# Softmax rows of two of four heads turned on VectorE in 32x32 blocks and put together by DMAs inside SBUF, instead of on TensorE

## What is computed

```python
# _L3_xattn_ref; _L2_xattn_ref has its own layernorm, a bias and a gate besides
q = (query @ w_q).reshape(B, Q, HEADS, HEAD_DIM).transpose(0, 2, 1, 3)
k = (key @ w_k).reshape(B, Kl, HEADS, HEAD_DIM).transpose(0, 2, 1, 3)
v = (value @ w_v).reshape(B, Kl, HEADS, HEAD_DIM).transpose(0, 2, 1, 3)
scores = jnp.einsum('bhqd,bhkd->bhqk', q, k) * scale
attn = jax.nn.softmax(scores, axis=-1)
out = jnp.einsum('bhqk,bhkd->bhqd', attn, v)
out = out.transpose(0, 2, 1, 3).reshape(B, Q, HEADS * HEAD_DIM)
return out @ w_o
```

## Time and profile before

| | |
|---|---|
| runs | 1220.64, 1214.82, 1216.54 us; median 1216.54 |
| span of the profiled execution | 1219.8 us, from its first to its last instruction |
| TensorE busy | 1054.1 us, 86% of the span |
| VectorE, ScalarE, GpSimd busy | 59%, 53%, 47% |
| steps 1 to 15 of attention 3 and 4 | about 549 to 720 and 895 to 1065 us |

### The profile page before, as it was taken

How to read it: one execution, slowest core, us unless ns; L and a number is a source line. 1 busy time by engine, 2 the same in 40 slices (tenths; PEclk the granted TensorE clock), 3 DMA queues, 4 the chain that set the end, 5 groups by cost and what they waited for, 6 DMA issues and landing times.

```text
span 1219.8 us, 22199 instructions
## 1 busy us (share of the span) xinstructions
PE 1054.1 (86%) x6815; PEld 797.4 (65%) x6815; DVE 717.3 (59%) x2444; ACT 643.9 (53%) x2117; POOL 571.5 (47%) x926
## 2 busy tenths in 40 slices
PE   4988999758889998979999987777799999977994
PEld 3865788735555667856767665566566776654994
DVE  5575354476776771386767784322876776852444
ACT  2244323357778723358778862222387888731321
POOL 5223655451000152566555656366375555655452
PEclk9987999989999988889999997697899999986997
DMA  2003556599600124110000001364300000014665
GB/s 63 13 27 112 161 165 208 163 156 385 237 1 1 36 68 137 54 30 19 1 19 19 1 5 43 85 187 121 87 19 1 2 1 1 2 33 129 200 208 173
DMA packets 116005, 102.87 MB, mean 84 GB/s; under 512 B 18027, under 2 KB 97571, under 8 KB 115888
## 3 DMA queue, kind: packets, MB, share of 16 engines
q1 hardware_dynamic: 105280, 82.71, 23.3%
q0 software_dynamic: 8448, 17.20, 4.2%
q10 hardware_dynamic: 2160, 1.53, 0.5%
HBM read 65.04 MB, written 36.36 MB: 83 GB/s over the span
## 4 chain that ended last, share of the span: by engine, by line
PE 61%; DVE 16%; issue 6%; ACT 5%; POOL 4%; DMA 4%; another core or an unknown queue 3%; SPq 2%; DVEq 0%; ACTq 0%; POOLq 0%
PE ps L2973 4%; PE ps L2777 4%; PE ps L2869 4%; PE ps L2882 4%; PE ps L2779 4%; PE ps L2778 4%; PE ps L2987 3%; PE ps L3515 3%; PE ps L3519 3%; PE ps L3168 2%; PE ps L3528 2%; PE ps L3001 2%; PE ps L3327 2%; ACT ex L1323 2%
## 5 line engine op out<-in xcount | busy, mean ns | idle before, releaser
L1323 ACT ACTIVATE ex<-ps,nmx 128x154 f32<-128x154 f32 x512 | 194.0, 391 | 75.0 <-DVE nmx L2278 73.2
L1085 POOL TENSOR_TENSOR pp<-ex,rc 128x256 f32<-128x256 f32 x256 | 157.6, 615 | 146.0 <-DVE rc L2283 145.0
L2278 DVE TENSOR_REDUCE nmx<-ps 128x2 f32<-128x308 f32 x256 | 119.6, 470 | 60.2 <-PE ps L2779 59.2
L922 POOL DMA_INDIRECT yq_d<-yq,ids_q x78 | 74.7, 957 | 79.4 <-DVE yq L2030 60.6
L2973 PEld LDWEIGHTS ps<-ident,pp 128*128 128x128 f32 x640 | 73.9, 142 | 55.5 <-POOL pp L1086 46.5
L2777 PE MATMUL ps<-kp,q_s 128*128 128x308 f32 x256 | 95.5, 373 | 15.1 <-ACT ex L1323 12.6
L1323 ACT ACTIVATION_READ_ACCUMULATOR ex<-ps,nmx 128x1 f32 x512 | 105.2, 205 | 0.0
L2973 PE MATMUL ps<-ident,pp 128*128 128x128 f32 x640 | 100.1, 280 | 2.8 <-POOL pp L1086 2.8
L1440 ACT ACTIVATE pe<-ps,nmx 128x154 f32<-128x154 f32 x256 | 84.9, 394 | 32.0 <-DVE nmx L2161 30.9
L892 POOL TENSOR_TENSOR ln_r<-ln_v,mhalf 128x4 f32<-128x4 f32 x32 | 32.7, 1021 | 105.4 <-DVE ln_v L1736 86.8
L2869 PE MATMUL ps<-xc_q,w_q 128*128 128x256 f32 (+1 forms) x276 | 63.6, 371 | 19.3 <-issue 11.5
(11 more groups left out here) (481 smaller groups left out, 2831.6 us busy)
## 6 DMA issues: line engine op xcount, KB each, us to landing
w_r<-in_L_ffn_W SPq DMA_DIRECT2D x69, 256.0 KB
xq_d<-blankq SPq DMA_DIRECT2D x4, 4160.0 KB, 23.8
w_q<-in_L_ffn_W SPq DMA_DIRECT2D x46, 256.0 KB
w_q<-in_L_ffn_w SPq DMA_DIRECT2D x46, 128.0 KB
xq<-xq_d SPq DMA_DIRECT2D x24, 130.0 KB
w_s<-in_L_ffn_W SPq DMA_DIRECT2D x8, 256.0 KB
w_e<-in_L_ffn_W SPq DMA_DIRECT2D x8, 256.0 KB, 5.2
acc<-yq_d SPq DMA_DIRECT2D x8, 256.0 KB, 4.6
```

Source lines behind the costliest of these rows:

```text
L922: pool.indirect_dma_start(yq_d[:, :], bass.IndirectOffsetOnAxis(ap=ids_q[:, c:c + 1], axis=0), yq[k % NY][:, h, :], None).then_inc(q_out[k ...
L1085: pool.tensor_tensor(pp[st % 2][:, m % 4, 2 * j:2 * j + 2, :], w[:, :, 0:P], r.broadcast_to([P, 2, P]), ALU.mult)
L1323: ins = act.activation(ex[:, tt % NEX, j, :], ps[:, tt % 3, j * SK:(j + 1) * SK], ACT.Exp, bias=nmx8[:, tt % 8, j:j + 1], accum_out=sm8[:, ...
L2278: dve.tensor_reduce(nmx8[:, tt % 8, :], ps[:, tt % 3, 0:2 * SK].rearrange("p (h s) -> p h s", h=2), AX.X, ALU.max, negate=True).then_inc(n ...
```

## The change

In steps 0 to 14 of both loops (`LAST_TURNED`) chunks 0 and 1 no longer go over TensorE and PSUM. Step 15 is as before.

- VectorE turns each of the two chunks with one instruction, `turn_blocks(st, c)`: 128 x 512 elements from `pp` into `pt_b`, in 32x32 blocks, each block staying on its 32 partitions. The first stands between the adding-up of the projection and `maxima(st, 6)`, the second behind `maxima(st, 6)`. Both wait until GpSimd has finished the step's first four units, and until the DMAs of the step before have landed, since `pt_b` exists once.
- SyncE moves the blocks to their partitions with 16 DMAs a step, `blocks_home`, each of 32 partitions x 2 chunks x 128 elements (32 KB), from `pt_b` to `pt_pair`. They wait for the second turn, and for `values(st - 1, 0)`, since `pt_pair` exists once too. All 16 count on one semaphore.
- TensorE loses 8 transposes a step, ScalarE the copy of chunk 0, VectorE the copy of chunk 1. `values(st, 0)` waits for all 16 DMAs, reads `pt_pair` with a pattern of runs of 32 elements, and moves from the middle of the next step to its end, behind `scores(st + 1, 7)`.
- The weight loads of SyncE are put between or behind the DMAs of certain steps. The ring of PSUM banks has two names less a step.

```diff
+    LAST_TURNED = NST - 2
+    def by_blocks(st, c):
+        return c < 2 and 0 <= st <= LAST_TURNED
...
+        pt_b = over("pt_b", [P, 2, S], F32, w1_at)[0]
+        pt_pair = over("pt_pair", [P, 2, S], F32, pt_at)[0]
...
+            def blocks_home(l, between):
+                for st in range(LAST_TURNED + 1):
+                    sp.wait_ge(*turned_blocks(l, st, 1))
+                    wait(sp, n_va, sides(l) + 2 * st - 1)
+                    for o in range(4):
+                        for a in range(4):
+                            sp.dma_start(pt_pair[32 * o:32 * o + 32, :, a * P:(a + 1) * P], pt_b[32 * a:32 * a + 32, :, o * P:(o + 1) * P]).then_inc(n_moved, 16)
+                    if st in between:
+                        raw_weights(*between[st])
...
-                raw_weights(2, (2, 3))
+                raw_weights(2, (2,))
...
-            raw_weights(3, (0, 1))
+            blocks_home(2, {2: (2, (3,)), 8: (3, (0,)), 12: (3, (1,))})
             region(2)
-            raw_weights(3, (2, 3))
+            raw_weights(3, (2,))
+            blocks_home(3, {2: (3, (3,))})
             region(3)
...
                 def copy_pt(st, c):
-                    if 0 <= st < NST:
+                    if 0 <= st < NST and not by_blocks(st, c):
...
+                def turn_blocks(st, c):
+                    if by_blocks(st, c):
+                        dve.wait_ge(n_z, base(l - 1, 8 * NST) + 8 * st + 4)
+                        if st or l > 2:
+                            dve.wait_ge(*moved_blocks(l, st - 1))
+                        dve.transpose(pt_b[:, c, :], pp[st % 2][:, :, c, :].rearrange("p t (o k) -> p o t k", o=4)).then_inc(n_turn, 1)
...
+                    turn_blocks(st, 0)
                     maxima(st, 6)
+                    turn_blocks(st, 1)
                     step_prep(st, 2)
...
                 def transposes(st, c):
-                    if not 0 <= st < NST:
+                    if not 0 <= st < NST or by_blocks(st, c):
                         return
...
-                    pe.wait_ge(*drained(l, RING[l][0]["pt", st, 2 * j]))
-                    pe.wait_ge(*drained(l, RING[l][0]["pt", st, 2 * j + 1]))
+                    if by_blocks(st, 2 * j):
+                        pe.wait_ge(*moved_blocks(l, st))
+                    else:
+                        pe.wait_ge(*drained(l, RING[l][0]["pt", st, 2 * j]))
+                        pe.wait_ge(*drained(l, RING[l][0]["pt", st, 2 * j + 1]))
...
+                        keys = pt_pair[:, h, :].rearrange("p (a t q) -> p t a q", a=4, t=TB) if by_blocks(st, h) else pt_s[h][:, :]
...
                     scores(st, 3)
-                    values(st - 1, 0)
                     transposes(st - 1, 3)
...
                     scores(st, 7)
+                    values(st - 1, 0)
                     values(st - 1, 1)
                     rest_values(st - 1)
```

More of the change, by code:

```diff
@@ L97, in behind, with turned @@
                 return BEHIND.get((st, at), [])
+            def turned(x, c):
+                return [] if by_blocks(x, c) else [("pt", x, c)]
             late, later = 0 < st, 2 <= st
-            names += [("pt", st - 1, 1)] * late + spot(0) + spot(1) + behind("A") + [("pt", st - 1, 2)] * late
+            names += turned(st - 1, 1) * late + spot(0) + spot(1) + behind("A") + [("pt", st - 1, 2)] * late
             names += [("pt", st - 1, 3)] * late + [("y", st - 2)] * later + [("pt", st - 1, 4)] * late + spot(2) + behind("C")
-            names += spot(3) + behind("D") + [("pt", st, 0)]
+            names += spot(3) + behind("D") + turned(st, 0)
         names += ENDING[l]
@@ L510, in xattn_moe_stack @@
         n_fin = sem("n_fin")
+        n_turn, n_wrote, n_moved = s_h, s_g, s_yp
         ROUTE_V = ("gr", 0), ("d", 0), ("oh", 0), ("kr", 0), ("place", 0), ("gr", 1), ("d", 1), ("oh", 1), ("kr", 1), ("place", 1), ("gr", 2), ("d", 2), \
@@ L546, in sides, with turned_blocks, wrote_blocks, moved_blocks @@
             return (0, 0, NST, 3 * NST)[l]
+        def turned_blocks(l, st, c):
+            return n_turn, 2 * NRUN + 2 * ((l - 2) * (LAST_TURNED + 1) + st) + c + 1
+        def wrote_blocks(l, st):
+            return n_wrote, 2 * NRUN + 32 * ((l - 2) * (LAST_TURNED + 1) + st + 1)
+        def moved_blocks(l, st):
+            return n_moved, NRUN + 256 * ((l - 2) * (LAST_TURNED + 1) + st + 1)
         def outs(l):
@@ L635, in xattn_moe_stack @@
         xq_d = [nc.dram_tensor(f"xq_d{l}", [EMPTY + RUN, XC], F32, kind="Internal").ap() for l in REGION]
+        pt_d = nc.dram_tensor("pt_d", [2 * P, S], F32, kind="Internal").ap()
         yq_d = nc.dram_tensor("yq_d", [SPARE + NRUN * RUN, D], F32, kind="Internal").ap()
@@ L2986, in values @@
                         h = 2 * j + i
-                        last = mm(ps[64 * i:64 * i + 64, 5 + j, :], vv[g % 2][:, b, 64 * h:64 * h + 64], pt_s[h][:, :], start=True, stop=False)
+                        keys = pt_pair[:, h, :].rearrange("p (a t q) -> p t a q", a=4, t=TB) if by_blocks(st, h) else pt_s[h][:, :]
+                        last = mm(ps[64 * i:64 * i + 64, 5 + j, :], vv[g % 2][:, b, 64 * h:64 * h + 64], keys, start=True, stop=False)
                     last.then_inc(n_va, 1)
```

## The result

The changed kernel takes 1273.41 us (median of 4 runs, 1270.45 to 1279.78), the kernel before 1217.81 in the runs beside it (4 runs, 1214.82 to 1220.64): a ratio of 1.0467, 95% interval 1.0429 to 1.0506, or +55.6 us. It is outside the range of 1190 to 1230, and on the other side of no change.

A forecast was written before the change was run, and what follows sets the result against it. TensorE was taken as the bound; each step becomes the longer of (before - 1.03) and 10.7 us. With 0.6 us charged at the loop's end: -8.9 a loop, -17.8 for both, median 1199 us, range 1190 to 1230.

The forecast's parts named there:

- the circle: Each step: 16 DMA issues, landing, first turn, maximum 6, second turn; 9.0 + 1.7 = 10.7 us, no step shorter.
- The last of 16 goes out 15 x 0.43 = 6.5 us after the first.: SyncE's block DMAs, each step: 0.43 us an issue, bounds 0.35 and 0.55, taken from rows of other DMAs.
- the rival of the longer circle: DMA issues, landing and turns take longer than 10.7 us; at 12.4 us a step, 1227 us in all; chance 0.22.
- the first step of each loop: Stretch from ScalarE's first exponential to the first `rest_values`; forecast to count nothing.
- The moved product: `values(st, 0)` on TensorE, moved to the next step's end: 0 us taken, at worst 15 us in all.
- The removal: Transposes of chunks 0 and 1 leave TensorE's chain: 0.59 + 0.44 = 1.03 us a step, in 30 steps.
- the wait for GpSimd that I had as a rival: VectorE or GpSimd take the chain, so TensorE's 1.03 us are not given back: 1208 or 1216 us; chance 0.20.
- Turns: Two on VectorE a step, 0.68 us each, hidden except at the loop's end, where 0.6 us is charged once.
- The pattern of runs of 32: TensorE's products reading `pt_pair`: no extra time taken; at worst twice as long, 0.5 us a step.
- Weight loads between: Four loads on SyncE, 1.7 us, fit in the 4.2 us in which it has nothing to issue; cost nothing.
- PEclk stays at 1.00: Sign of a right forecast: TensorE keeps 2.4 GHz, as in all earlier steps, even one with 0.8 us idle.
- DMAs one after another: Each block DMA lands before the next moves: 40 us in place of 9.0, about 2050 us; chance 0.02.

The follow-up runs named there:

- turns alone: Changed kernel with both VectorE turns in every step but the 16 block DMAs in step 0 of each loop alone: 1227.21 us, ratio 1.0049.
- removed only: Changed kernel with turns and block DMAs in step 0 of each loop alone, product still at the step's end: 1219.69 us, ratio 0.9998.

## Why the prediction was wrong

From median to median the 55.6 us are: the removal -15.2 (from 14 steps a loop, where the change has 15), the move of the product +9.8, the turns with a trip through DRAM -0.2, the 16 DMAs in place of that trip +61.1. Each term has 5 to 6 us to either side; that they add up proves nothing, since each kernel is compared with the next. Where the circle sets the steps, the product's place is hidden by it, so these terms hold for this order alone.

- **The step that failed: "The last of 16 goes out 15 x 0.43 = 6.5 us after the first."** It took 15 x 0.64 = 9.6. The rows from which I took 0.43, and 0.55 as the upper bound, are loads from DRAM. I had named the lack of a row with both ends in SBUF as an argument for a rival, and still kept 0.55 as the bound. The other two terms of the circle were near: landing 1.85 for 2.5, turns with the maximum 1.87 for 1.73. 13.3 in place of 10.7. It was the rival of the longer circle that came true, with the signs that I had named for it, and its own price of 24 us for each microsecond above 12.5 gives 1227 + 0.8 x 24 = 1246. The 27 us that are left are about what the windows hold beyond 13.3 us a step, by three things that no price of mine had: the first step of each loop, of which I had said that it counts nothing, +9.3; three steps of 17.8 us with stretches at 1.2 GHz, 4.5 each above the circle; eight circles with one long issue, 0.8 to 1.3 each. None of the three was measured by a run of its own.
- **With the predicted circle the forecast would have failed too.** 12 DMAs make just that circle, 10.7 us, and 1231 us, not 1199; even without the first step, in which that run keeps all 16, its windows are 1.4 us above before, not 17.8 below. Two more terms were off. *The moved product, "I take nothing"*, costs 9.8: I had looked at the length of its instructions and not at the wait that it filled. *The removal* gives 15.2, or 17.3 by the windows, where 1.03 in every step but the last two of a loop made 25: 12.48 became 11.65, but 14.10 became 13.73. The 1.03 was read from the chain and is too much: TensorE's busy time falls by 11.2 us in 14 steps of attention 3, 0.80 a step. And 2.5 of these 11.2 become longer waits, above all the wait for GpSimd that I had as a rival: 2.9 us in a loop with the removal alone, 0.6 before. Of the 19 us between the medians with 12 DMAs and through DRAM, 6 are in the first steps and 6 in the windows. That is nearly all by which the two profiled executions differ, 12.4; the rest is in no profile and stays open.
- **Turns: right in size.** 0.70 us each for 0.68, and hidden in most steps. At the loop's end they show, as forecast, but with more than the 0.6 us that I had charged: against the kernel with removal and move the two windows there are 2.2 and 1.2 us longer in the two loops, part of it a fall of the clock. The medians say 7.5 us for the turns in one pair of kernels (turns alone against removed only) and nothing in the other (through DRAM against removal and move). The estimate of 1.24 from the Trainium skill ("VectorE: DVE Perf Modes", section "The three transpose paths") is not borne out for 128x512 elements of fp32.
- **The pattern of runs of 32: right.** Four products take 1.08 us with it at full clock, where four from `pt_s` take 1.03 to 1.08.
- **Weight loads between: right.** They went out while SP waited for the turns, from 580.41 to 582.36 us, with the next block DMA at 583.44.
- **"PEclk stays at 1.00": wrong.** That the clock stayed up at a wait of 0.8 us told nothing of waits of 3 us, and in some steps it fell behind waits of 0.7 and 1.0 us.
- **DMAs one after another:** no; 16 issues and one landing. What the Trainium skill says in "DMA: Bandwidth & Descriptors", section "Anatomy of one DMA — SWDGE (gpsimd) path", that a DMA from GpSimd has a fixed cost of about 2 us whatever its size, is near the landing of 1.85 us for 32 KB on SP's queue, though that is another queue.
- **One row was misread.** The last window of the earlier trace rows ends at 719.50, but that step's `rest_values` starts at 720.11. The forecast counts nothing there, so its sum is the same.

## What to carry to other kernels

Price a DMA by its place in the queue: n small ones issued in a row have (n - 1) issues ahead of the landing, and where each buffer exists once, that sum and all that refills the buffer is the shortest step. Take the issue from a row with the same ends (SBUF or DRAM) or give it a range wide enough to cross the threshold, and try fewer, larger DMAs first, even by way of DRAM. Before moving work that "costs the same anywhere", look which wait it fills where it stands. An experiment that is free of the cost in steady state can still pay it once at the start, so compare windows as well as medians; and when windows are compared, set those apart in which the granted clock fell.

## What the runs showed of the hardware

- An issue on SP from SBUF to SBUF, 32 partitions, 32 KB, takes 0.60 us, with 64 pieces of 512 bytes as with 32 of 1 KB (0.59), and 0.04 passes to the next. Writes of a chunk to DRAM take 0.34, reads of 256 pieces of 512 bytes 0.45. Nine on the chain of the changed kernel's two loops take 1.2 to 1.7 us; what stops them is not shown.
- Such a DMA lands 1.9 us after its issue in the median (1.8 to 3.2), the read from DRAM after 2.8 (2.3 to 3.9).
- VectorE turns 128x512 fp32 in 32x32 blocks in 0.70 us; a copy of as many elements takes 0.68.
- TensorE fell to 1.2 GHz behind a wait of 3.02 us, and also behind two waits for ScalarE of 0.72 and 0.98 us (step at 636.90; the same two waits stand ahead of the fall in the kernel with removal and move, which has no DMAs there). But equal waits did not always bring a fall. In the changed kernel the step at 554.14, behind a wait of 3.07 us, kept the full clock. And in seven other profiles, of kernels without these transposes, with the product at the end and without a circle that sets the steps (removed only, removed and moved, 8 and 12 DMAs, three through DRAM), the two steps a loop that took 14.10 before have these two waits each time, 0.71 to 0.73 and 0.97 to 0.98 us: the clock fell in 10 of 28, for some 1.6 us (14.57 to 16.15), and stayed up in 18.
